# A state-space scan on one NeuronCore: step size folded into the decay's exponent, query and key sums in one product of 32 rows

## What is computed

```python
xn = layernorm_over_channels(x)
z, xBC, dt = split(in_proj_w @ xn)              # 256, 320, 8
xs, B, C = split(silu(depthwise_conv3x3(xBC)))  # 256, 32, 32
dt = softplus(dt + dt_bias);  A = -exp(A_log)   # 8 heads
# 1024 tokens of an image in 8 chunks of 128, per head h:
Acs = cumsum(dt * A)                            # within the chunk
Ldec[q, s] = exp(Acs[q] - Acs[s]) if s <= q else 0
Y = (C @ B.T * Ldec) @ (xs * dt) + exp(Acs) * (C @ state)
state = exp(Acs[-1]) * state + (B * exp(Acs[-1] - Acs)).T @ (xs * dt)
y = rmsnorm((Y + D * xs) * silu(z));  x = x + out_proj_w @ y
```

## Time and profile before

| | us |
|---|---|
| three runs, median | 2383.64 (2360.32, 2383.64, 2384.04) |
| the profiled execution, its own time | 2373.73 |
| its span in the trace | 2372.0 |
| PE / DVE / ACT / POOL busy | 2151.1 / 1654.6 / 1266.2 / 1526.2 |
| the chunk loop: first and last start of L467 | 84.4 and 695.6 |

### The profile page before, as it was taken

One profiled execution on the slowest core, in us unless ns is written; L12 is line 12 of the kernel. 1 busy time (PEld: TensorE's weight loads), 2 busy tenths in 40 slices (PEclk: granted clock), 3 DMA queues, 4 the chain that ended last, 5 costly groups with the idle time before them and its releaser, 6 DMA issues. The chain is left out here.

```text
span 2372.0 us, 39890 instructions
## 1 busy us (share of the span) xinstructions
PE 2151.1 (91%) x11907; PEld 1749.7 (74%) x11907; DVE 1654.6 (70%) x4242; ACT 1266.2 (53%) x2623; POOL 1526.2 (64%) x1473
## 2 busy tenths in 40 slices
PE   4799998999995999999999999999999993799993
PEld 2466666666674888888888888888888882688883
DVE  4778976877846677777877878778777773344444
ACT  3556555555531666666666666666666661233331
POOL 2678866866841666677686785867868675355551
PEclk9988988898885999999999999999999996899995
DMA  1950000000000001010010010100101001455555
GB/s 62 387 185 10 10 10 1 10 1 1 1 19 19 10 1 26 1 27 18 4 41 1 11 35 1 43 2 8 37 1 41 5 7 41 171 191 189 198 170 213
DMA packets 135401, 130.93 MB, mean 55 GB/s; under 512 B 82885, under 2 KB 101359, under 8 KB 135190
## 3 DMA queue, kind: packets, MB, share of 16 engines
q1 hardware_dynamic: 124950, 107.12, 14.8%
q0 software_dynamic: 9088, 17.07, 2.1%
q10 hardware_dynamic: 1152, 4.19, 0.4%
HBM read 64.78 MB, written 65.10 MB: 55 GB/s over the span
## 5 line engine op out<-in xcount | busy, mean ns | idle before, releaser
L1219 POOL TENSOR_TENSOR plo<-pf,phi 128x512 fp32r<-128x512 f32 (+1 forms) x640 | 752.0, 1187 | 340.2 <-ACT phi L1447 311.2
L1445 ACT ACTIVATE pf<-psum 128x512 f32<-128x512 f32 (+1 forms) x640 | 357.1, 558 | 412.9 <-PE psum L1280 310.6
L1447 ACT ACTIVATE phi<-psum 128x512 fp32r<-128x512 f32 (+1 forms) x640 | 355.1, 555 | 0.0
L1591 DVE CUSTOM_DVE_ANT_0 psum<-psum,ahead_wide 128x128 f32<-128x128 f32 (+3 forms) x512 | 246.8, 503 | 70.1 <-PE psum L1333 68.5
L1278 PE MATMUL psum<-phi,x_tok 128*128 128x512 f32 (+1 forms) x640 | 265.8, 415 | 5.8 <-POOL plo L1219 5.8
L1872 POOL DMA_INDIRECT chosen<-yg,xg x156 | 152.8, 979 | 154.2 <-DVE yg L1984 109.3
L1333 PE MATMUL psum<-xT,qT 128*128 128x512 f32 (+3 forms) x768 | 246.0, 349 | 3.8 <-DVE peak L1591 3.4
L1278 PE MATMUL psum<-qT,xT 128*128 128x512 f32 (+1 forms) x640 | 238.1, 372 | 1.1 <-DMA qT<-nmax 0.6
L1279 PE MATMUL psum<-plo,x_tok 128*128 128x512 f32 (+1 forms) x640 | 237.6, 371 | 0.0
L1280 PE MATMUL psum<-phi,x_tok 128*128 128x512 f32 (+1 forms) x640 | 237.4, 371 | 0.0
L1279 PE MATMUL psum<-qT,xT 128*128 128x512 f32 (+1 forms) x640 | 236.8, 370 | 0.0
(11 more groups left out here) (291 smaller groups left out, 5306.3 us busy)
## 6 DMA issues: line engine op xcount, KB each, us to landing
wg<-turned_w SPq DMA_DIRECT2D x39, 874.0 KB, 4.6
...
qT<-nmax SPq DMA_DIRECT2D x512, 0.5 KB, 2.0
...
```

The lines of the kernel that those rows point to most:

```text
L1219: g_.tensor_tensor(plo[:, T % RP, 0:n], pf[:, T % RF, 0:n], phi[:, T % RP, 0:n].bitcast(F32), ALU.subtract).then_inc(a["low_ready"], 1)
L1445: s_.activation(pf[:, T % RF, 0:n], bank[T % RS][:, 0:n], ACT.Exp)
L1447: s_.activation(phi[:, T % RP, 0:n], bank[T % RS][:, 0:n], ACT.Exp).then_inc(a["high_ready"], 1)
L1591: last = v.tensor_tensor_reduce(out=source[:, col:col + n], in0=source[:, col:col + n], in1=ahead_wide[:, HALF - n:HALF], scale=1.0, scala ...
```

## The change

The step size leaves the data: instead of multiplying xs by dt, the logarithm of dt is added to the exponent of the decay on the key's side. POOL's product `xdt` goes, and `tok` itself is the operand of `chunk_y` and of `Xd`. The sums at query and key, high and low parts, lie in 32 rows a chunk (4 kinds x 8 heads), four chunks over 128 partitions, two halves an image. One product of 32 rows replaces the two of 128 rows in each bank. To make them: ACT takes Ln of dt (`log_of_steps`, place 2), DVE spreads it (`logs`, place 3), PE turns the sums (`turn_sums`, end of place 4, through `spare`), ACT copies (`high_sums`), DVE splits (`split_sums`, place 5), ACT writes two operands (`set_sums`, place 5), POOL spreads them over heads (`spread_sums`, places 6 and 1). `halves` and `apart` go. The layer norm of the next image (`normalise`) moves on ACT from place 6 to place 5, `turn_back(nn, 0)` on PE ahead of `chunk_turn` in place 6, `spread_bc` ahead of `pad_copy(nn, 0)` on ACT, and one tap of the convolution from place 5 to place 4 on DVE. Core of the diff:

```diff
+    def spread_sums(n, half):
+        pool.wait_ge(s["sums_set"], n + 1)
+        need(pool, "seg_ready", (n - 1) * NC + 4 * (half + 1))
+        g_.tensor_tensor(by_query[:, half, :, :], at_query[:, half, :].unsqueeze(1).to_broadcast([P, NH, P]),
+                         of_head[:, :].unsqueeze(2).to_broadcast([P, NH, P]), ALU.mult).then_inc(s["sums_spread"], 1)

...
         n, nn, j = front(step)
         if 0 <= step - 1 < G:
             chunk_end(step - 1)
-        if 0 <= step < G:
-            chunk_in(step)
         if 0 <= step - 2 < G:
             chunk_gate(step - 2)
...
             if j == 6:
                 silu_bc(n)
+                spread_sums(n, 0)
             if j == 7:
                 silu_x(n, 1)
         if has(nn) and j == 4:
             deviation(nn)
+        if has(n - 1) and j == 1:
+            spread_sums(n - 1, 1)
...
     def cumulate(n):
         need(pe, "state_ready", states[0])
         pe.wait_ge(s["dA_ready"], n + 1)
-        t.matmul(bank[5][:, DI:DI + NC * NH], upto[:, :], dA[:, n % 2, 0:NC * NH], start=True, stop=True)
-        t.matmul(bank[5][0:NS, DI + NC * NH:DI + 2 * NC * NH], ones_col[:, 0:1].to_broadcast([P, NS]), dA[:, n % 2, 0:NC * NH],
-                 start=True, stop=True)
-        t.matmul(bank[5][:, 384:512], dA[:, n % 2, :], upto[:, :], start=True, stop=True).then_inc(s["acs_ready"], 1)
+        t.matmul(bank[5][:, DI:DI + NC * NH], upto[:, :], dA[:, :, 0, :], start=True, stop=True)
+        t.matmul(bank[5][0:NS, DI + NC * NH:DI + 2 * NC * NH], ones_col[:, 0:1].to_broadcast([P, NS]), dA[:, :, 0, :],
+                 start=True, stop=True).then_inc(s["acs_ready"], 1)
+
+    def turn_sums(n):
+        spare_free("sums_low", n + 1)
+        pe.wait_ge(s["log_less"], n + 1)
+        for half in range(2):
+            to = spare[:, half * P:(half + 1) * P]
+            t.matmul(to, dA[:, 4 * half:4 * half + 4, :, :].rearrange("p c k h -> p (c k h)"), upto[:, :], start=True, stop=False)
+            last = t.matmul(to, less_log_flat[:, half, :], ident[:, :], start=False, stop=True)
...
         n, c = g // NC, g % NC
-        if c == 0:
-            pe.wait_ge(s["sums_apart"], n + 1)
+        if c % 4 == 0:
+            pe.wait_ge(s["sums_set"], n + 1)
+            pe.wait_ge(s["sums_spread"], 2 * n + c // 4 + 1)
+        mine = slice(32 * (c % 4), 32 * (c % 4) + 32)
         need(pe, "decay_ready", g)
         for j in range(2):
             seg = bank[2 + j][:, :].rearrange("p (h q) -> p h q", q=P)
             t.matmul(seg, ident_bf[:, :], mask_after[:, :].unsqueeze(1).to_broadcast([P, 4, P]), start=True, stop=False)
-            t.matmul(seg, halves[:, n % 2, :], minus_one[:, c, 4 * j:4 * j + 4].unsqueeze(2).to_broadcast([P, 4, P]),
-                     start=False, stop=False)
-            last = t.matmul(seg, group_ones[:, 2 * c + j:2 * c + j + 1].to_broadcast([P, P]), apart[:, n % 2, :, :], start=False, stop=True)
+            last = t.matmul(seg, by_key[mine, n % 2, c // 4, :], by_query[mine, c // 4, 4 * j:4 * j + 4, :], start=False, stop=True)
         last.then_inc(s["seg_ready"], 1)

...
             if j == 4:
                 project_z(n - 1, 3)
-        if has(nn) and j == 2:
-            residual(nn, 0)
+        if has(nn):
+            if j == 2:
+                residual(nn, 0)
...
-        if has(nn):
-            if j == 6:
-                turn_back(nn, 0)
-            if j == 7:
-                project(nn, 0)
+        if has(nn) and j == 7:
+            project(nn, 0)
         if 0 <= step - 3 < G:
             chunk_out(step - 3)
         if has(n):
...
                 project(n, 3)
             if j == 1:
                 project(n, 5)
+            if j == 4:
+                turn_sums(n)
         if has(nn):
             if j == 2:
                 residual(nn, 1)
...
+        need(act, "sums_set", n)
...
+    def log_of_steps(n):
+        act.wait_ge(s["dA_ready"], n + 1)
+        need(act, "log_less", n)
+        a_.activation(log_dt[:, :], dt[:, n % 2, :], ACT.Ln, bias=least[:, 0:1]).then_inc(s["log_ready"], 1)
+
+    def high_sums(n):
+        act.wait_ge(s["sums_turned"], n + 1)
+        a_.activation(sum_high.bitcast(F32R), spare[:, 0:2 * P].rearrange("p (a q) -> p a q", q=P), ACT.Copy).then_inc(s["sums_high"], 1)
+
+    def set_sums(n):
+        act.wait_ge(s["sums_split"], n + 1)
+        need(act, "sums_spread", 2 * n)
+        need(act, "seg_ready", (n - 1) * NC)
+        a_.activation(at_query[:, :, :], sum_part, ACT.Identity, scale=is_query[:, 0:1], bias=not_key[:, 0:1])
+        a_.activation(by_key[:, n % 2, :, :], sum_part, ACT.Identity, scale=is_key[:, 0:1], bias=is_query[:, 0:1]
+                      ).then_inc(s["sums_set"], 1)
+
...
-        if has(nn) and j == 2:
-            residual(nn, 0)
+        if has(nn):
+            if j == 2:
+                residual(nn, 0)
+            if j == 6:
+                turned_back(nn, 0)
         if 3 <= step < G + 6:
             chunk_out(step)
-        if has(nn) and j == 6:
-            normalise(nn, 0)
-            normalise(nn, 1)
-            turned_back(nn, 0)
         if has(n):
             if j == 1:
                 soft_plus(n)
+            if j == 2:
+                log_of_steps(n)
+            if j == 5:
+                set_sums(n)
             if j == 4:
                 decay_in(n)
             if j in WEIGH:
...
                 tanh_x(n, 0)
             if j == 6:
                 tanh_bc(n)
-        if has(nn) and j == 7:
-            pad_copy(nn, 0)
         if has(n) and j == 7:
             spread_bc(n)
+        if has(nn):
+            if j == 5:
+                normalise(nn, 0)
+                normalise(nn, 1)
+            if j == 7:
+                pad_copy(nn, 0)
         if 0 <= step - 2 < G:
...
     def decays(n):
         dve.wait_ge(s["dtln_ready"], n + 1)
-        need(dve, "xdt_ready", (n - 1) * NC)
+        need(dve, "log_ready", n - 1)
         link(v.scalar_tensor_tensor(dt[:, n % 2, :], dtr[:, :], 0.0, dtl[:, :], ALU.max, ALU.add))
-        need(dve, "acs_ready", n - 1)
-        v.tensor_tensor(dA[:, n % 2, :].rearrange("p (k c h) -> p k c h", c=NC, h=NH),
-                        dt[:, n % 2, :].rearrange("p (c h) -> p c h", h=NH).unsqueeze(1).to_broadcast([P, 2, NC, NH]),
-                        aneg[:, :].unsqueeze(1).unsqueeze(1).to_broadcast([P, 2, NC, NH]), ALU.mult
+        need(dve, "sums_turned", n)
+        v.tensor_tensor(dA[:, :, :, :], dt[:, n % 2, :].rearrange("p (c h) -> p c h", h=NH).unsqueeze(2).to_broadcast([P, NC, 4, NH]),
+                        aneg[:, :].unsqueeze(1).unsqueeze(1).to_broadcast([P, NC, 4, NH]), ALU.mult
                         ).then_inc(s["dA_ready"], 1)
+
+
+    def logs(n):
+        dve.wait_ge(s["log_ready"], n + 1)
+        if n + 1 < B:
+            need(dve, "tb_ready", 2 * (n + 1))
+        v.tensor_tensor(less_log, log_dt[:, :].rearrange("p (c h) -> p c h", h=NH).unsqueeze(2).to_broadcast([P, NC, 4, NH]),
+                        minus_key[:, :].unsqueeze(1).unsqueeze(3).to_broadcast([P, NC, 4, NH]), ALU.mult
+                        ).then_inc(s["log_less"], 1)
+
+    def split_sums(n):
+        dve.wait_ge(s["sums_high"], n + 1)
+        link_low = v.tensor_scalar(sum_part, spare[:, 0:2 * P].rearrange("p (a q) -> p a q", q=P), is_low[:, 0:1], None, ALU.mult)
+        link_low.then_inc(s["sums_low"], 1)
+        dve.wait_ge(s["sums_low"], n + 1)
+        v.scalar_tensor_tensor(sum_part, sum_high, sign[:, 0:1], sum_part, ALU.mult, ALU.add).then_inc(s["sums_split"], 1)

     def cumulated(n):
         dve.wait_ge(s["acs_ready"], n + 1)
-        need(dve, "decay_ready", (n - 1) * NC)
         need(dve, "eacs_ready", n - 1)
-        need(dve, "seg_ready", (n - 1) * NC)
-        link(v.tensor_copy(halves[:, n % 2, :], bank[5][:, 384:512]))
-        v.tensor_tensor(halves[64:P, n % 2, :], bank[5][64:P, 384:512], halves[64:P, n % 2, :].bitcast(F32), ALU.subtract)
         need(dve, "edec_ready", n)
         v.tensor_copy(totals[:, :], bank[5][0:NS, DI + NC * NH:DI + 2 * NC * NH])
         v.tensor_scalar(nAcs[:, n % 2, :], bank[5][:, DI:DI + NC * NH], -1.0, None, ALU.mult).then_inc(s["nacs_ready"], 1)
-
-    def sums_apart(n):
-        dve.wait_ge(s["nacs_ready"], n + 1)
-        need(dve, "seg_ready", (n - 1) * NC)
-        v.tensor_tensor(apart[:, n % 2, :, :], halves[:, n % 2, :].bitcast(F32).unsqueeze(1).to_broadcast([P, 4, P]),
-                        of_four[:, :].unsqueeze(2).to_broadcast([P, 4, P]), ALU.mult).then_inc(s["sums_apart"], 1)

...
     TAPS_AT = {0: ((0, range(0, 3)),), 1: ((0, range(3, 6)),), 2: ((0, range(6, 9)),), 3: ((1, range(0, 1)),),
-               4: ((1, range(1, 3)),), 5: ((1, range(3, 6)),), 6: ((1, range(6, 9)),)}
+               4: ((1, range(1, 4)),), 5: ((1, range(4, 6)),), 6: ((1, range(6, 9)),)}
     for step in range(FIRST, LAST):
...
+            if j == 3:
+                logs(n)
             if j == 4:
                 cumulated(n)
+            if j == 5:
```

(1 more changed line is left out.)

85 lines of the change are left out of this document (46 added, 39 removed).

## The result

The changed kernel takes 2461.76 us (median of 4 runs, 2440.12 to 2481.31), the kernel before 2381.31 (4 runs, 2360.32 to 2384.04): ratio 1.033, 95% interval 1.022 to 1.043. The forecast was 2346, its range ended at 2385. The profiled execution took 2454.8, its span 2453.0 (before 2372.0). Some executions of any kernel here run slower at a lower granted clock, such as the 2481.31 above and the profiled ones of experiments 2 and 3d; the ratios leave them out, so a ratio can stand lower than two medians suggest.

The account below looks back on a forecast made before the run. PE sets the pace where fed, DVE close behind; POOL's queue and the clock in places 5 and 6. Per image 63.4 work + 6.1 idle + 10.0 half clock = 79.5, 3.5 less; seven images -24.5, last -3.6: 2346, range 2298 to 2385.

Parts of the forecast that it names:

- The exponent: PE, all 8 steps of an image: one product fewer per bank, 16 x 0.225 = 3.6 us saved; lower bound nothing gained.
- Half clock as before, 10.0: Per image: 10.0 us lost to PE's half clock stays, since idle time is as long and only lies elsewhere.
- The slower rival: Waits at places 3 and 4 put PE on half clock there: 2391 for one place, 2437 for two; chance 0.12.
- behind the first two waits: Kernel before: clock falls to half behind PE's waits of 0.86 us on DVE (place 4) and 1.62 on `Xd` (place 5).
- work saved is time saved: Ledger per image: PE work falls from 66.0 to 63.4 us and counts in full towards 3.5 us less length.
- The last image: Eighth image, no front work: steps PE-bound at 6.6 us, each 0.45 shorter, 3.6 us saved in all.
- DVE holds it: Rival: saved PE time turns into waits for DVE and POOL, nearly full in places 1 and 4; 2360, chance 0.20.
- The wait at `turn_sums`: End of place 4: PE waits for `zs`, DVE's last operation there, 2.6 us, bounds 1 and 4.
- Place 3: PE's `project_z` waits for ACT's second residual copy, queued behind `log_of_steps`: 1.5 us, bounds 0 and 3.
- Place 6: PE's wait for `Xd`: 1.5 us instead of 2.8, bounds 0 and 4, without `xdt` in POOL's queue.
- The boundary wait: Before the next image's first chunk: PE's 1.39 us goes, as `spread_bc` no longer stands behind `pad_copy`.
- DVE, a term mis-sized: Small operations per image: three go, four of about 0.3 to 0.6 us come; net zero, bounds -0.5 and +0.8.

Follow-up runs that it names:

- experiment 2: Kernel before, one of its two sum products cut to the chunk's 32 rows, three products a bank as before: 2485.75 us, ratio 1.048.
- 3d: Changed kernel with the exponent product over the 64 rows of two chunks instead of 32: 2426.53 us, ratio 1.022.
- (b) of experiment 3: Changed kernel with its 32-row product issued twice in a row in each bank: 2467.94 us, ratio 1.037.
- experiment 1: Changed kernel with the new exponent product over all 128 rows instead of 32, decay not the reference's: 2371.28 us, ratio 1.002.
- Experiment 4: Kernel before without its first exponent product (L479), two full products a bank instead of three: 2369.76 us, ratio 1.001.
- 7: Kernel before with the change's order of work, `silu_x` of half 0 on POOL in place 6, and without L479's product: 2341.08 us, ratio 0.989.
- 8: Changed kernel over 128 rows and right, ScalarE writing each chunk's key side with zeros outside its 32 rows: 2367.14 us, ratio 0.999.
- 5: Kernel before with only the change's order of work (`normalise` in place 5, `turn_back` and `spread_bc` ahead), three full products: 2349.26 us, ratio 0.992.
- 9: As 8, with the logarithm behind the second residual copy and the tap back in place 5: 2356.70 us, ratio 0.996.
- 10: As 9, with `turn_sums` in the middle of place 4 and the z projection behind it: 2374.69 us, ratio 1.004.
- 3c: Changed kernel with the mask product issued twice in each bank: 2451.22 us, ratio 1.035.
- 6: Kernel before with the change's order of work and `silu_x` of half 0 moved on POOL from place 5 to 6: 2344.12 us, ratio 0.989.

## Why the prediction was wrong

**The exponent, the step that failed.** "Whether the product of 32 rows costs as little as one of 128 rows no row shows ... Bounds: as the removed product of 128 rows, or as the two it replaces." The value lay outside both bounds. -3.6 us an image was forecast; by rows 1.49 against 1.35 it is 8 x 0.14 = +1.1. The 32-row product behind one of its own kind costs 0.23, the time of one of 128 rows, as the rule of the Trainium skill says that I leaned on (TensorE: Matmul & The Clock Gate, "Why this matters for your kernels"), and (b) of experiment 3 agrees: 0.23. What neither the rule nor my bounds held is the neighbour: each change of row count lays a weight load bare, 0.14 us net in the mean, four a step. The upper bound should have had that load in full, which the earlier trace rows could not exclude and which loads such as L503's at 688.28 in the kernel before hinted at.

**"Half clock as before, 10.0", the second failure and the larger.** It is 0.16 x 85.4 = 13.7 in the image shown, 124.0 instead of 59.1 over seven, and image 0 at half clock for 67 us on top. With full rows (experiment 1) the loss is 63.1 over seven: it is the 32-row product that brought it. The slower rival had the clock as the place of the loss and the sign right (0.12), but not the cause: it put the fall down to the waits of places 3 and 4. Experiment 1 has these waits, up to 2.1 and 2.3 to 2.6 us, and its clock is 0.88; experiment 2 has none of them and is 116 us slower than before. The reading that the clock falls "behind the first two waits" was wrong too: in the earlier trace rows place 4, with its wait of 0.86, has clock 1.00.

**The ledger's rule that work saved is time saved.** Experiment 4 shows it false for this loop even with a full product: -29 us of work, no gain (0.999 to 1.004); 7 points the same way. The last image, which I took as bound by PE with 0.45 us off each step, gives 0.20 (6.63 to 6.43 in 1 and 4). The rival "DVE holds it", 2360 at 0.20, was nearer for a cheap product (1 and 8: 2371 and 2367), and of the two the better account: of experiment 1's waits 11.8 us end with DVE's `zs`. But 10.4 end with ACT's residual copy and 17.5 with POOL's `Xd`, so it is not DVE alone.

**Right.** The wait at `turn_sums`, 2.64 against 2.6, ended by `zs`. That it fits so well is in part luck: `zs` came later by `logs` (below), and PE likely came later by its dearer exponent. Place 3: 1.06 in two images, 2.08 where PE is fast (1), against 1.5 (0 to 3). Place 6: 1.0 against 1.5. The boundary wait is gone. `turn_sums` takes 502.05 - 500.18 = 1.87 us, near the bound of +1.5 net once 0.4 is taken off for the product it replaces (L445); but it stands right behind its wait and runs at half clock (0.50 over 499.80 to 502.05), which the forecast's +1.0 did not have. POOL is level, 60.11 against 60.24. ACT's loads take 1.28 and the next activation follows at once (the load at 482.95, `Ldec` at 484.24): no drain, so the 1.38 us of the Trainium skill (ScalarE: Activation LUTs, "What ACT_TABLE_LOAD costs") is again not in the trace.

**DVE, a term mis-sized.** It is 1.8 us an image busier, outside my bounds of -0.5 to 0.8. Most of that is `logs`, put at 0.3 "about as long as dA": it takes 0.43 at best and 1.57 in the middle of its eight. In place 3 of the fifth image it starts just behind a sum on POOL and ends just behind that sum's end (start, length):

```profile
482.83 1.37 POOL L318 TENSOR_TENSOR accC<-accC,tapC 128x544 f32<-128x544 f32 x1
482.91 1.57 DVE L909 TENSOR_TENSOR xt<-log_dt,minus_key 128x256 f32<-128x256 f32 x1
```

These rows agree with the rule of the Trainium skill on the shared port (SBUF — State Buffer, "SBUF: two separate sides"), by which one of the two engines waits for the other's whole instruction; here DVE was the one that lost. No experiment isolates it.

**The order of work** is worth 20 us (5); I had it inside the waits of place 6 and the boundary, at 7 x (1.3 + 1.4) = 19. So what of the forecast 28 came true came from the order, not from the folded step size.

**What stays open.** Why the granted clock stays at half for 12 us steps in which PE's records have no gap. It goes with changes of row count within the exponent: none, first clock record at 86 to 91 and 40 to 72 us lost over images 1 to 7 (85 and 92 in the two versions of 9 and 10); two, 87 and 108, with image 0 at a mean of 0.70; four (the change, 3b, 3c), 134 to 152 and 113 to 128. That the laid-bare loads are idle time of the array that no busy share shows is argued, not shown; so is the rival, that the clock goes by how many rows of the array are used (3d is in its range, 3b and 3c don't decide). No run varies bare loads and rows used apart from each other. And why 7 lost 32 us more to the clock than 6 in the executions profiled, with a product less, is not settled either.
